# Token attention's modulation in seven vector instructions, with the row maximum taken by the multiplication

## The reference, cut to what matters

```
qkv  = x @ W_qkv + b_qkv;  q, k, v = split(qkv)
attn = (q @ k^T) * SCALE                        # 512 x 512 scores for each batch
xn   = sigmoid(attn)
mult = 2.0 if xn > 0.95, 1.5 if xn > 0.85, 0.1 if xn < 0.1, 0.3 if xn < 0.25, else 1.0
attn = softmax(attn * mult)
out  = (attn @ v) @ W_proj + b_proj
```

## Time and profile before

| what | value |
|---|---|
| median of 3 runs | 577.84 us (575.66 to 580.05) |
| span of the profiled execution | 573.3 us |
| instructions in it | 7484 |
| DVE busy | 496.8 us, 87%, 938 instructions |
| PE busy | 499.5 us, 87%, 2224 instructions |
| ACT busy | 342.9 us, 60% |
| POOL busy | 333.1 us, 58% |

### The profile page before, as it was taken

The page is one execution under the profiler, slowest core; times in us unless marked ns, Lnnn a source line. Parts: engine busy times, 40 slices in busy tenths (PEclk is TensorE's granted clock), DMA queues, the critical chain, the costliest instruction groups (busy, mean ns, idle before and its releaser), DMA issues.

```text
span 573.3 us, 7484 instructions
## 1 busy us (share of the span) xinstructions
PE 499.5 (87%) x2224; PEld 384.0 (67%) x2224; DVE 496.8 (87%) x938; ACT 342.9 (60%) x581; POOL 333.1 (58%) x275
## 2 busy tenths in 40 slices
PE   3678899999989779998779997779997999999996
PEld 2455677788757657776557775666775777677883
DVE  3557999697899999999997999988999779798875
ACT  3454774767646678557566557565584655745563
POOL 4324778765745556754655455563465647677673
PEclk9789998999989998999888999989997999999999
DMA  8400000000000000000000000000000000000000
GB/s 269 144 2 1 1 1 1 0 2 0 1 0 2 1 0 1 2 0 1 2 0 1 0 2 1 0 1 1 2 18 1 1 1 19 1 1 2 18 2 18
DMA packets 7780, 7.44 MB, mean 13 GB/s; under 512 B 700, under 2 KB 7612, under 8 KB 7740
## 3 DMA queue, kind: packets, MB, share of 16 engines
q1 hardware_dynamic: 7740, 6.97, 3.8%
HBM read 5.91 MB, written 1.05 MB: 12 GB/s over the span
## 4 chain that ended last, share of the span: by engine, by line
PE 46%; DVE 38%; issue 9%; ACT 4%; POOL 2%; DMA 1%; SPq 0%; DVEq 0%; ACTq 0%; POOLq 0%
PE bank L890 12%; PE bank L892 11%; PE bank L891 11%; DVE alo L834 8%; DVE t L827 6%; DVE xn L699 4%; PE bank L1062 2%; DVE mk L860 2%; DVE bst L685 2%; DVE mk L855 2%; DVE mk L851 1%; DVE bmx L864 1%; ACT ah L600 1%; PE bank L984 1%; PE bank L1053 1%
## 5 line engine op out<-in xcount | busy, mean ns | idle before, releaser
L497 POOL TENSOR_TENSOR t<-t,sl 128x512 f32<-128x512 f32 x168 | 261.7, 1568 | 176.7 <-DVE t L827 165.2
L834 DVE TENSOR_TENSOR alo<-t,ah 128x512 fp32r<-128x512 f32 x168 | 160.5, 955 | 33.3 <-ACT ah L600 32.7
L594 ACT ACTIVATE sl<-bank 128x512 f32<-128x512 f32 x168 | 100.4, 598 | 91.2 <-POOL t L497 72.6
L600 ACT ACTIVATE ah<-t 128x512 fp32r<-128x512 f32 x168 | 105.7, 629 | 68.2 <-PE bank L892 67.6
L827 DVE TENSOR_TENSOR t<-bank,sbc 128x512 f32<-128x512 f32 x168 | 113.9, 678 | 3.9 <-PE bank L892 3.9
L890 PE MATMUL bank<-xhF,WUh 128*128 128x512 f32 x168 | 71.2, 424 | 24.1 <-DVE t L827 24.0
L890 PE MATMUL bank<-xhF,WGh 128*128 128x512 f32 x168 | 76.8, 457 | 0.1
L890 PE MATMUL bank<-ah,WDh 128*128 128x512 f32 x168 | 69.0, 411 | 4.3 <-DVE alo L834 2.4
L892 PE MATMUL bank<-xhF,WUl 128*128 128x512 f32 x168 | 68.4, 407 | 0.0
L892 PE MATMUL bank<-xhF,WGl 128*128 128x512 f32 x168 | 68.2, 406 | 0.0
L891 PE MATMUL bank<-xlF,WUh 128*128 128x512 f32 x168 | 68.2, 406 | 0.0
(11 more groups left out here) (168 smaller groups left out, 800.5 us busy)
## 6 DMA issues: line engine op xcount, KB each, us to landing
stage<-in_gate SPq DMA_DIRECT2D x7, 192.0 KB, 6.2
stage<-in_up SPq DMA_DIRECT2D x7, 192.0 KB, 6.3
stage<-in_down SPq DMA_DIRECT2D x7, 192.0 KB, 6.2
X<-in_x SPq DMA_DIRECT2D x4, 256.0 KB, 5.6
out<-X SPq DMA_DIRECT2D x4, 256.0 KB, 2.3
raw<-in_small SPq DMA_DIRECT2D x1, 580.0 KB
rows<-in_row SPq DMA_DIRECT2D x1, 136.0 KB, 5.8
cols<-in_columns SPq DMA_DIRECT2D x1, 3.0 KB
```

What stands on the lines that cost most here:

```text
L497: pool.tensor_tensor(t2[k % NT2][:, :], t2[k % NT2][:, :], sl[k % NSL][:, :], ALU.mult).then_inc(a_done, 1)
L594: act.activation(sl[k % NSL][:, :], bank[k % 2][:, :], ACT.Silu).then_inc(silu_done, 1)
L600: act.activation(ah[k % 2][:, :], t2[k % NT2][:, :], ACT.Copy).then_inc(ahi_done, 1)
L834: dve.tensor_tensor(alo[k % 2][:, :], t2[k % NT2][:, :], ah[k % 2][:, :].bitcast(F32), ALU.subtract).then_inc(alo_done, 1)
```

## The change

The multiplier minus one was a sum of four steps (2, 7, 5, 5); it is now max(1 + 2a, 10b) + 5(c + d) for the four compares a to d, which gives the same 1, 3, 10, 15, 20. Part 0 ends in one scalar_tensor_tensor in place of a tensor_tensor. Part 1 has one compare, and a scalar_tensor_tensor that does the other compare and the addition. Part 2 is one scalar_tensor_tensor on the bf16 tiles in place of two instructions. Part 3 is a tensor_tensor_reduce that multiplies `Sb` by the multiplier, writes `Sb`, and takes the row maximum into a new tile `bmp`; a tensor_scalar on 128 x 1 negates it into `bmx`. `COST` of the step is .8 in place of .9; `plan()` gives the same list of 1053 steps for both.

```diff
--- before.py
+++ after.py
@@ -104,7 +104,7 @@
             asim=(1.3, 0, 0), ass=(0, 0, .1), ascale=(0, 0, .3), asT=(.1, 0, 0), amax=(0, 0, .5), aexp=(0, 3, 0),
             aT=(.1, .2, .1), aav=(.9, .5, 0), y=(.9, 0, .6), route=(2, 1.1, .3), rexp=(0, 2.7, 0),
             rsum=(0, 0, 1.3), rrank=(0, 0, 1.1), tanh=(0, .5, 0), gelu=(0, 0, .6), act=(.9, 0, 0), actk=(0, 0, 1.3),
-            sbc=(.4, .5, 0), yT=(.4, 0, .6), bqk=(.7, 1, 0), bs=(.7, .5, 0), bsp=(0, 0, .9),
+            sbc=(.4, .5, 0), yT=(.4, 0, .6), bqk=(.7, 1, 0), bs=(.7, .5, 0), bsp=(0, 0, .8),
             bv=(.7, 0, .6), bexp=(0, 1.2, 0), bpT=(.4, .5, 0), bo=(.9, .1, 0),
             by=(.9, 0, 0), byx=(0, 0, 1.4))
 DEBT = 0.1
@@ -326,7 +326,7 @@
         mk = [sb(f"mk{i}", [P, T], BF16) for i in range(4)]
         PT = sb("PT", [P, NT, T])
         oT = sb("oT", [P, T])
-        bmx = sb("bmx", [P, NT])
+        bmx, bmp = sb("bmx", [P, NT]), sb("bmp", [P, NT])
         brs = sb("brs", [P, NT])
         bri = sb("bri", [P, NT])
         bt = sb("bt", [P, NT, D])
@@ -849,19 +849,21 @@
                     if part == 0:
                         wait_free(dve, turn_of["bs", b, i])
                         dve.tensor_scalar(mk[0][:, :], x_, X10 / 10, 2.0, ALU.is_ge, ALU.mult)
-                        chain(dve.tensor_scalar(mk[1][:, :], x_, X25 / 10, 7.0, ALU.is_ge, ALU.mult))
-                        dve.tensor_tensor(mk[0][:, :], mk[0][:, :], mk[1][:, :], ALU.add).then_inc(mk_ready, 1)
+                        chain(dve.tensor_scalar(mk[1][:, :], x_, X25 / 10, 10.0, ALU.is_ge, ALU.mult))
+                        dve.scalar_tensor_tensor(mk[0][:, :], mk[0][:, :], 1.0, mk[1][:, :], ALU.add, ALU.max)\
+                           .then_inc(mk_ready, 1)
                     if part == 1:
-                        dve.tensor_scalar(mk[2][:, :], x_, X85 / 10, 5.0, ALU.is_gt, ALU.mult)
-                        chain(dve.tensor_scalar(mk[3][:, :], x_, X95 / 10, 5.0, ALU.is_gt, ALU.mult))
-                        dve.tensor_tensor(mk[2][:, :], mk[2][:, :], mk[3][:, :], ALU.add).then_inc(mk_ready, 1)
+                        chain(dve.tensor_scalar(mk[2][:, :], x_, X95 / 10, None, ALU.is_gt))
+                        dve.scalar_tensor_tensor(mk[3][:, :], x_, X85 / 10, mk[2][:, :], ALU.is_gt, ALU.add)\
+                           .then_inc(mk_ready, 1)
                     if part == 2:
                         dve.wait_ge(mk_ready, step_no + 2)
-                        chain(dve.tensor_tensor(mk[0][:, :], mk[0][:, :], mk[2][:, :], ALU.add))
-                        dve.scalar_tensor_tensor(x_, mk[0][:, :], 1.0, x_, ALU.add, ALU.mult).then_inc(mk_ready, 1)
+                        dve.scalar_tensor_tensor(mk[0][:, :], mk[3][:, :], 5.0, mk[0][:, :], ALU.mult, ALU.add)\
+                           .then_inc(mk_ready, 1)
                     if part == 3:
                         dve.wait_ge(mk_ready, step_no + 3)
-                        dve.tensor_reduce(bmx[:, i:i + 1], x_, AX_X, ALU.max, negate=True).then_inc(sp_ready, 1)
+                        chain(dve.tensor_tensor_reduce(x_, mk[0][:, :], x_, 1.0, -3e38, ALU.mult, ALU.max, bmp[:, i:i + 1]))
+                        dve.tensor_scalar(bmx[:, i:i + 1], bmp[:, i:i + 1], -1.0, None, ALU.mult).then_inc(sp_ready, 1)
                 if kind == "bpT" and s[2] == 0:
                     dve.wait_ge(bexp_done, NT * (s[1] + 1))
                     dve.reciprocal(bri[:, :], brs[:, :])
```

## The result

The changed kernel takes 583.86 us in the median of 9 runs (581.16 to 584.47), the kernel before 577.86 (575.51 to 582.97). The ratio is 1.0079, with a 95% interval of 1.0047 to 1.0111: slower by 4.6 us (2.7 to 6.4). The two medians lie 6.0 us apart, inside that interval. The ratios here are formed from the fast runs, without those of a slower state of the chip (584.05 us at a granted clock of 0.936 for e3_half_steps, say), and not from the medians. The profiled execution spans 579.4 us in place of 573.3.

What follows compares the result with a forecast made beforehand. PE (46%) and DVE (38% of the span) were taken to bound the kernel in turns. On the path, +0.8 us of instructions and +3.6 of waits made +4.4 on 577.84: 582.2 us, range 576 to 589.

Steps and rivals of the forecast that it cites:

- Two turns, PE and DVE: Whole kernel: PE (46% of the chain) and DVE (38%) bound it in turns; DVE time counts only in DVE's stretches.
- Part 0, +0.27: Part 0 on DVE: the bf16 addition (0.34) becomes a scalar_tensor_tensor at L861's price, +0.27 us each, 3.5 on the path.
- third rival: Parts 0 and 2: the bf16 scalar_tensor_tensor runs as fast as the bf16 addition, giving 575.2 us; chance 0.10.
- Part 1, -0.07: Part 1 on DVE: two compares and an addition (1.12) become a compare and a scalar_tensor_tensor (1.05), -0.9 us on the path.
- part 2, -0.45: Part 2 on DVE: the chained addition goes and one scalar_tensor_tensor stays, -0.45 us each, -5.9 on the path.
- Part 3, +0.29: Part 3 on DVE: reduction (0.60) becomes main instruction 0.61, accumulator read 0.21, negation 0.07; +0.29 us each, 4.1 on the path.
- two-pass rival: Part 3: the new reduction takes two passes, 1.21 for 0.61 us, giving 590.6 us; chance 0.18.
- Waits of part 3, +3.6 on the path: Part 3's reduction, now with two SBUF inputs, waits for POOL's running L497; seven of 16 blocks meet it, +3.6 us.
- Off-path waits at nothing: Part 3 waits at 215.0 and 299.3, where PE has the chain or is about to, count 0; 2.2 us kept for the range.
- PE's clock at nothing: PE stretches: no cost counted; a clock falling for longer or shorter there was named as a sign of being wrong.
- No gain at all without waits, +0.04 a block: Parts 0 to 3 on DVE: the four price changes sum to +0.04 us a block, +0.8 us on the path.
- theory A: DVE start-to-start costs count where DVE has the chain; two-SBUF-input instructions or compares behind a pair wait for POOL's L497, reductions don't.

Runs made afterwards that it cites:

- e3_half_steps: Against the kernel before: part 3 as in the change with scale 2.0, a 1 moved into the first compare as 0.5, all sums tensor_tensor; ratio 0.9937, -3.6 us.
- e7: The kernel before with only part 0's sum made a scalar_tensor_tensor in place of the tensor_tensor, same values; ratio 1.0106, +6.1 us.
- e4: The kernel before with the same instructions, only the product of Sb and multiplier moved from part 2 to in front of part 3's reduction; ratio 1.0099, +5.7 us.
- e1: The changed kernel with parts 0 and 1 as before the change; ratio against the kernel before 1.0022, +1.3 us.
- e2: The changed kernel's sums with the old reduction in part 3 and a separate product in part 2; ratio against the kernel before 1.0144, +8.3 us.
- e5: e3_half_steps with reduction and negation moved into part 2 right behind the sum, part 3 empty; ratio against the kernel before 1.0003, +0.2 us.
- e6: The kernel before with its reduction moved into part 2 behind the product, part 3 empty; ratio 1.0117, +6.8 us.

## Why the prediction was right, and where it was lucky

The forecast was 582.2 us, +4.4; the median is 583.86. The timed ratio gives +4.6, the medians +6.0, and the traces +4.0 to chunk 120 and +6.0 to the end. Step by step:

- **Two turns, PE and DVE.** Right for DVE as far as tried: all eleven kernels change DVE's program alone, and eight of them move the time beyond their interval, by up to 11.6 us. That PE's turns cost nothing did not hold; see the point on PE's clock.
- **Part 0, +0.27, by L861's price and not by the bf16 addition's.** Right: 691 ns and 691 to 694 after. The third rival is out by this row. Its price on the path was 3.5 us; e7 has 3.6 in the trace, 6.1 timed (4.3 to 7.9).
- **Part 1, -0.07; part 2, -0.45.** Instruction by instruction right: 691 to 693 ns for the scalar_tensor_tensor of part 1, and one instruction in part 2. By themselves they were not timed.
- **Part 3, +0.29.** The main instruction was right, 0.61 from start to start. The accumulator read was mis-sized: I took 0.21, it costs 0.11 (206.24 to 206.36). So part 3 costs +0.20, 14 x 0.09 = 1.3 us less than in the sum. The two-pass rival is out by the minimum of 657.
- **Waits of part 3, +3.6 on the path.** The mechanism was right and is shown by e4, where the old product takes the wait in that place. The count was near: five waits of 1.1 us, where the forecast had four full ones in front of a pair (three came), two shortened by 0.5 (they came, at 174.9 and 288.5), and one of 0.2 (it didn't). The one at 416.5 is the one I read at 413.7; of those four the one at 215 did not come. Of the signs foretold, POOL's two L497 no longer stand together behind part 3 in three of the four places, and still do at 215. DVE's busy time rose by 4.2 us and not by 6: these two waits and the cheaper read are 1.1 + 0.2 + 16 x 0.09 = 2.7 us less. What is left is a net of several: the first compare of part 1 lasts 1.1 us longer in all than before (13.8 for 12.6) and a comparison of the router, L786, 1.0 longer, while `alo` lasts 2.9 less.
- **Off-path waits at nothing.** In the change this was right as far as seen: at 215 the wait didn't come, and the one at 300.1 moved nothing (+0.8 us at chunk 76 in front of it, +0.8 at chunk 84 behind it). In e4 the same place adds about 1.2 (+1.8 and +3.0).
- **PE's clock at nothing.** This is the term that the sum lacked, though the prediction names it among the signs of being wrong. It lets DVE's stretches bring all of the +4.4, and PE's none. In the trace about +1.4 of the +4.0 come between chunks 99 and 105 (378.1 to 398.8 before), where the chain is PE's. The rest, in the other stretches together, is +2.6. Behind the blocks the 2.0 us of chunks 144 to 150 follow. In both places the granted clock is lower in the changed kernel; for the first, before and then the changed kernel:

```profile
378.00:399.00 21.00, 20.22 (x92) 15.24 (x92) 17.85 (x35) 12.50 (x21) 9.91 (x7) 0.92 0.00 0
379.50:402.00 22.50, 21.72 (x91) 16.59 (x92) 18.14 (x33) 12.50 (x21) 9.48 (x7) 0.86 0.00 0
```

The same work keeps PE busy 1.5 us longer. So the size is right partly by luck: the other stretches brought 1.8 us less than the forecast, of which the dear accumulator read explains 1.3, and PE's stretch with the lower clock brought 1.4. That the change is slower is not luck. Whether the longer waits on DVE make the clock fall, or whether it falls there by chance in this one execution, no run here separates.

- **No gain at all without waits, +0.04 a block.** Right in kind: e1 and e2 undo one half each, and neither is faster than before. It is the step that carries the result, by e7 and e3: three cheap additions of 0.34 were traded for dear ones of 0.61.
- **How good the sums of theory A are.** To chunk 120 the traces lie within 0.8 us of them for after, e1, e2, e5, e6 and e7; e3 is 1.8 faster and e4 2.2 slower. Timed, the kernels forecast slower came out slower than their sums: e2, e4, e6 and e7 by 2.4 to 4.7 us. The clock is a candidate for the difference and is not tried: within one kernel the longer runs show the lower granted clock (e3: 571.8 to 574.1 us at 0.955 to 0.964, 579.6 and 579.8 at 0.941), so a median depends on how often it falls.

The rule of the Trainium skill on the scalar_tensor_tensor shape ("Vector Engine (DVE) Microarchitecture Reference", Points that are easy to get wrong) does not show in the plain instruction. The kernel has one with two f32 tiles in SBUF, outside the change, in before:

```profile
L799 DVE SCALAR_TENSOR_TENSOR hq<-hq,xa x8: 682/684/1179, 42.8 to 505.1; 50x512 f32<-50x512 f32 x8
```

Its 512 columns take 684 ns in the median, no more than the 691 of L861 with one bf16 source. For the reduction, which has an accumulator, the rule was not tried: one source was bf16 in all these kernels. The Performance modes list of the same page of the Trainium skill agrees with the trace: 691 ns for the bf16 scalar_tensor_tensor, 424 for the tensor_tensor.

## What to carry to other kernels

Count microseconds from start to start, not instructions: on these bf16 tiles two tensor_tensor cost less than 0.7 us and one scalar_tensor_tensor 0.6, and here the fusion paid only where it took away a pass over f32 data without making a cheap pass dear, as e3_half_steps does by moving a constant into a compare. Before fusing an instruction away or moving it, ask what runs beside it: the reduction that stood where POOL held the port cost 0.1 of its 0.6 us in the place shown, and the fused one stands and waits in its place. And when a wait is moved to another place in a row, follow what is queued behind it: here the next wait was PE's, for `alo`. When sums and times differ by a microsecond or two, compare the granted clock stretch by stretch before looking for a wait that was missed.

## What the runs showed that I had not expected

- DVE and POOL don't always decide alike who goes first: with the same 0.44 us between the starts, DVE waits 1.1 us at 288.5 and passes at 215.3, and in e4_product_moved it passes in the same block, at 219.4.
- The first 155 us, the same on DVE in all these kernels, took 155.2 to 160.2 us in the profiled executions; PE's granted clock over them was 0.94 before, where they took 155.2, and 0.90 in e4_product_moved, where they took 160.2. The runs of one kernel spread by 3 to 12 us, and a part of that scatter may be made there.
- PE's granted clock falls in different places in different kernels, and one such fall, between 500 and 525 us in seven of the twelve kernels, costs 2.1 us, half as much as the whole change does in its 16 blocks.
